# Reordering the prologue of an AdaLN block: modulation, filler matmuls, vector loads and a GpSimd subtraction

## The reference

```python
mod = (silu(c) @ wmod).reshape(4, 6, 1, 256)          # c is (4, 256), wmod is (256, 1536)
sa, ca, ga, sb, cb, gb = (mod[:, k] for k in range(6))
ga, gb = bounded(ga), bounded(gb)
h = layernorm(x) * (1 + ca) + sa
x = x + ga * mixer(h)          # first half
h = layernorm(x) * (1 + cb) + sb
x = x + gb * experts(h)        # second half: 8 experts, top 2, FFN width 1024

def mixer(x):
    xn = rmsnorm(x, norm1_w)
    left = gelu(xn @ left_W + left_b)
    u = causal_conv4(xn @ right_W + right_b)
    r, i = sigmoid(u @ ga_W + ga_b), sigmoid(u @ gx_W + gx_b)
    log_a = -8 * softplus(a_param) * r
    h = linear_recurrence(exp(log_a), sqrt(1 - exp(2 * log_a)) * i * u)
    x1 = (left * h) @ out_W + out_b + x
    x1n = rmsnorm(x1, norm2_w)
    return (gelu(x1n @ up1_W + up1_b) * (x1n @ up2_W + up2_b)) @ down_W + down_b + x1
```

## Time and profile before

| | us |
|---|---|
| median of 3 runs | 278.48 (278.12 to 279.31) |
| the profiled execution | 278.96 |
| its span, first to last instruction | 277.2 |

### The profile page before, as it was taken

How to read it: one execution, slowest core, us unless ns; L and a number is a source line. 1 busy time by engine, 2 the same in 40 slices (tenths; PEclk the granted TensorE clock), 3 DMA queues, 4 the chain that set the end, 5 groups by cost and what they waited for, 6 DMA issues and landing times.

```text
span 277.2 us, 4511 instructions
## 1 busy us (share of the span) xinstructions
PE 261.6 (94%) x1593; PEld 219.4 (79%) x1594; DVE 196.4 (71%) x459; ACT 173.7 (63%) x295; POOL 124.8 (45%) x104
## 2 busy tenths in 40 slices
PE   6989999899999999999999789999999999999991
PEld 2755655366688788877579689999999999999991
DVE  3678589919947777879947679885868677785630
ACT  4228778676189336990789557948669393958310
POOL 8140403000061302448275543877483838668454
PEclk9959999999999999999999999999999999999997
DMA  6990000000003857225277558869294875818044
GB/s 185 379 352 8 0 1 0 0 2 0 0 2 100 279 165 187 22 90 182 109 231 226 155 175 254 223 183 314 58 328 119 248 212 167 232 18 218 12 53 51
DMA packets 32838, 38.40 MB, mean 139 GB/s; under 512 B 7964, under 2 KB 28444, under 8 KB 32796
## 3 DMA queue, kind: packets, MB, share of 16 engines
q1 hardware_dynamic: 27184, 30.56, 35.6%
q0 software_dynamic: 4928, 7.44, 11.8%
q10 hardware_dynamic: 700, 0.07, 0.2%
HBM read 32.10 MB, written 8.90 MB: 148 GB/s over the span
## 4 chain that ended last, share of the span: by engine, by line
PE 63%; DVE 13%; ACT 7%; DMA 6%; issue 5%; POOL 4%; POOLq 1%; SPq 0%; DVEq 0%; ACTq 0%
PE bank L1008 18%; PE bank L1051 12%; PE bank L691 11%; PE bank L616 4%; PE bank L788 4%; POOL x_rows L2070 3%; PE bank L1045 2%; PE bank L1044 2%; DMA x_rows<-h_rows,slot_b 2%; PE bank L995 2%; DVE u L1577 2%; PE bank L627 2%; PE bank L635 1%; ACT tmp L1233 1%; DMA x_tok<-in_L_attn_x 1%
## 5 line engine op out<-in xcount | busy, mean ns | idle before, releaser
L2111 POOL DMA_INDIRECT out_x<-y_tok,meta x24 | 50.8, 2115 | 36.2 <-DVE y_tok L1938 20.9
L1051 PE MATMUL bank<-w_hi,own 128*128 128x256 f32 x256 | 48.2, 283 | 0.0
L1377 ACT ACTIVATE own_raw<-bank,b1c 128x320 f32<-128x320 f32 x64 | 33.4, 533 | 14.1 <-PE bank L1008 13.8
L1920 DVE TENSOR_TENSOR own<-own_raw,own 128x256 fp32r<-128x256 f32 x64 | 27.2, 425 | 20.0 <-ACT own L1383 19.9
L1051 PEld LDWEIGHTS bank<-w_hi,own 128*128 128x128 f32 x256 | 40.9, 191 | 0.0
L1008 PE MATMUL bank<-xe_hi,w_hi 128*128 128x320 f32 x128 | 39.9, 312 | 1.0 <-DVE xe_lo L1916 1.0
L1008 PE MATMUL bank<-xe_lo,w_hi 128*128 128x320 f32 x128 | 39.6, 309 | 0.0
L1008 PE MATMUL bank<-xe_hi,w_lo 128*128 128x320 f32 x128 | 39.6, 309 | 0.0
L1051 PE MATMUL bank<-w_lo,own 128*128 128x256 f32 x128 | 36.2, 283 | 0.0
L2101 POOL DMA_INDIRECT gb_rows<-gb_table,meta x24 | 24.9, 1037 | 12.3 <-issue 6.7
L1383 ACT ACTIVATE own<-own_raw 128x320 fp32r<-128x320 f32 x64 | 29.8, 482 | 0.0
(11 more groups left out here) (248 smaller groups left out, 606.2 us busy)
## 6 DMA issues: line engine op xcount, KB each, us to landing
e_raw<-in_L_ffn_w SPq DMA_DIRECT2D x16, 1024.0 KB, 5.8
x_rows<-in_L_attn_x SPq DMA_DIRECT2D x1, 2560.0 KB
xe_tok<-x_rows SPq DMA_DIRECT2D x7, 256.0 KB, 6.0
raw_m<-in_L_attn_up_W SPq DMA_DIRECT2D x2, 768.0 KB, 9.8
x_tok<-in_L_attn_x SPq DMA_DIRECT2D x2, 512.0 KB, 5.3
out_x<-x_tok SPq DMA_DIRECT2D x1, 1024.0 KB, 5.2
xe_tok<-x_rows SPq DMA_DIRECT2D x7, 128.0 KB, 6.2
wmod<-in_L_wmod SPq DMA_DIRECT2D x1, 768.0 KB, 11.7
```

What stands on the lines that cost most here:

```text
L1051: ins = nc.tensor.matmul(bank[b][0:n, 0:D], l, r, start=False, stop=(c == KE - 1 and t == 2))
L1377: nc.scalar.activation(own_raw[:, f % 4, :], bank[b][:, 0:CAP], ACT.Gelu, bias=b1c[:, g:g + 1]).then_inc(drained[b], 1)
L1920: nc.vector.tensor_tensor(own_lo[e % 2][:, f, :], own_raw[:, f % 4, 0:whole], own_hi[e % 2][:, f, 0:whole].bitcast(F32), ALU.subtract)
L2111: nc.gpsimd.indirect_dma_start(out_rows, bass.IndirectOffsetOnAxis(ap=ids[0:n, e, k, E:E + 1], axis=0), y_tok[e % 2][0:n, k, :], None, com ...
```

## The change

Five edits:
- Modulation: `warm(("warm", 1), ...)` moves from behind the wait for `cT` to ahead of it and has 4 fillers instead of 8; VectorE copies cT between `bn_stats` and `aggregate` instead of behind `aggregate`.
- Fillers: two between the blocks of the first mean square, two behind "vec", four instead of one behind the first `spread`.
- The even vectors are issued by ScalarE in three groups: two vectors behind a_param, two behind the sigmoid, three behind `ln_root(1)`.
- The last product of `left` of half 1 is split around `mean_square` of the second rmsnorm: its first matmul stands between the two blocks, its second behind them; `spread2(0)` comes ahead of "gb" and "b1"; one filler instead of four.
- GpSimd waits for the convolution of half 0 (`conv_done` at 2) before the first `wm_lo`.

```diff
-            def mean_square(key, hf, n):
+            def mean_square(key, hf, n, between=None):
...
+                    if between and dt == 0:
+                        between()
...
             transposes("cT", lambda j: c_row[0:B, j * P:(j + 1) * P], KD, B, step=B)
+            warm(("warm", 1), 4)
             until_drained("cT")
...
-            warm(("warm", 1), 8)
             pe.wait_ge(wmod_in, 16)
...
+            def fill(n):
+                ps = bank[order.at[("warm", 2)][0]]
+                for k in range(n):
+                    nc.tensor.matmul(ps[:], all_ones[:], all_ones[:, 0:1].to_broadcast([P, HT]), start=True, stop=True)
-            mean_square(("ms", 0), 0, 0)
+            mean_square(("ms", 0), 0, 0, lambda: fill(2))
...
             transposes("vec", lambda j: rows[0:NV, :], 1, NV)
+            fill(2)
             pe.wait_ge(rinv_done, 1)
             spread(("rb", 0), 0)
-            warm(("warm", 4), 1)
+            warm(("warm", 4), 4)
...
-            side("left", 1, 1, [1])
-            mean_square2(0)
+            left_bank, left = begin(("left", 1, 1))
+            def last_left(c):
+                return nc.tensor.matmul(left[:], raw_a[:, 1, c, P:2 * P], xn[:, c, hs[1]], start=(c == 0), stop=(c == KD - 1))
+            mean_square(("ms2", 0), 0, 2, lambda: last_left(0))
+            end(last_left(1), left_bank)
+            spread2(0)
...
-            any_w = wm_hi[:, 0]
-            spread2(0)
-            stay_busy(("busy", 5), any_w, 4)
-            wm_ready(2)
+            stay_busy(("busy", 5), wm_hi[:, 0], 1)
...
+            load_vectors(act, names[0:4:2], vec_in)
             act.wait_ge(consts_done, 2)
             act.wait_ge(c_in, 16)
             nc.scalar.activation(c_sig[0:B, :], c_row[0:B, :], ACT.Sigmoid).then_inc(sigmoid_done, 1)
+            load_vectors(act, names[4:8:2], vec_in)
...
-            load_vectors(act, names[0::2], vec_in)
+            load_vectors(act, names[8::2], vec_in)
...
-            ln_stats(x_tiles(0))
+            first_stats = bn_stats_of(x_tiles(0))
             b, ps = full("cT")
             nc.vector.tensor_copy(cT[:], ps[:, 0:KD * B].rearrange("p (k b) -> p k b", k=KD)).then_inc(drained[b], 1)
+            aggregate(x_tiles(0), first_stats)
...
+            pool.wait_ge(conv_done, KH)
             for n in range(2):
                 pool.wait_ge(wm_hi_done, n + 1)
                 lo(wm_lo[:, n], raw_m[:, n], wm_hi[:, n], wm_lo_done)
```

More of the change, by code:

```diff
@@ L1454, in bn_stats_of @@
                 return st.mark(last)
-            def ln_stats(tile):
-                aggregate(tile, bn_stats_of(tile))
             def x2_stats(hf):
```

## The result

| | before | changed |
|---|---|---|
| median of the executions beside each other | 279.23 us (278.12 to 281.45) | 277.0 us (275.72 to 280.7) |
| the profiled execution | 278.96 | 276.33 |
| its span | 277.2 | 274.6 |

The ratio is 0.9919, with a 95% interval of 0.9895 to 0.9943: faster by 0.8%, where 1.6% was forecast. The forecast of 274.1 missed by 2.9 us; 277.0 lies inside the range, close to the 276.0 of the rival in which the clock falls all the same. Of the 2.9 us, 0.75 are the level of the kernel before, whose median was 278.48 in the 3 runs shown and is 279.23 in 22; the gain was 2.2 us where 4.35 was forecast. (Ratios leave out executions over 1.5% above the fastest of their kernel, here four of the changed kernel's 22, at 280.2 to 280.7 us.)

What follows compares the result with a forecast made beforehand. It saw a sparse prologue chain, TensorE usually last, with the clock halved from 14.4 to 21.2. Gains of 0.95 + 1.0 + 1.95 = 3.9, plus 0.45, made 4.35 us: forecast 274.1, range 273.2 to 277.3.

Steps and rivals of the forecast that it cites:

- the clock falls all the same: Rival: prologue clock drops about when it did before; 277.9 us, or 276.0 if fillers bring it back; chance 0.3.
- Do they hold it?: Whether the prologue's new fillers keep the clock at full speed through spread and first side; given 0.63.
- the spread: First rmsnorm's spread, 8 matmuls: at held clock 1.05 us in place of 2.09, gaining 1.0.
- start of the spread: First rmsnorm's spread begins 0.95 us earlier, from the modulation's 1.3 less the fillers' overrun.
- the first side: First large product, 8 matmuls: at held clock about 3.5 us in place of 5.42, gaining 1.95.
- Modulation: Prologue's 16 small matmuls start about 6.8 in place of 8.22; xhat transposes end 1.3 us earlier.
- Fillers' overrun: New prologue fillers outlast their waits by about 0.25 us in the mean square and 0.1 behind "vec".
- The row that the 0.63 leaned on: Stretch at 58.2 in the kernel before: one-column matmuls mixed with wider ones, and the clock kept.
- Lock at softplus: GpSimd's moved subtraction holds softplus's first VectorE operation about 0.85 us, so half 1's gates start 0.55 late.
- GpSimd's wait: Moving the subtraction behind the convolution spares VectorE's xhat a hold that would cost at the new pace; no size.
- Second rmsnorm: Split left product and earlier spread bring xn 1.0 us earlier; 0.45 net of the late gates.
- That a gain at xn reaches the end: After the second rmsnorm VectorE carries the chain, so xn's gain, 4.35 us in all, is passed on.

Runs made afterwards that it cites:

- filled kernel: Changed kernel with seven single fillers through the first mean square in place of two, and six in place of four ahead of it: 275.13 us, ratio 0.9856.
- e4: Kernel before with only the second rmsnorm's edits (split left product, earlier spread, one filler in place of four): 278.46 us, ratio 0.9974.
- e14: Kernel before with only GpSimd's wait for the convolution ahead of the first wm_lo: 279.69 us, ratio 1.0016.
- e7: Filled kernel with the second rmsnorm back in the old order (whole left product, later spread, four fillers): 276.15 us, ratio 0.9886.
- e6: Filled kernel without GpSimd's wait for the convolution: 276.63 us, ratio 0.988.
- e11: Filled kernel with single fillers only in the first block of the first mean square, four in place of seven: 274.51 us, ratio 0.9833.
- e2: The run of the filled kernel: 275.13 us, ratio 0.9856.
- e9: The changed kernel itself, unaltered, run again for a second profile: 275.87 us, ratio 0.9873.
- e5: Changed kernel with the first mean square, root and reciprocal done 512 columns wide, no first spread, ten fillers in the wait for xn: 278.34 us, ratio 0.9961.
- e10: Kernel before with dense fillers alone, in the first mean square, ahead of it, behind vec and behind the spread: 279.23 us, ratio 0.9992.
- e3: Changed kernel without GpSimd's wait for the convolution: 277.24 us, ratio 0.9899.
- e12: Filled kernel with all seven even vectors issued behind the first root again: 276.6 us, ratio 0.9877.
- e1: Changed kernel without the prologue's new fillers (none in the mean square or behind vec, one behind the spread): 277.75 us, ratio 0.9929.

## Why the prediction was wrong

The step that failed is **"Do they hold it?"**, the 0.63 for the fillers holding the clock. They did not hold it: the clock was at 0.50 from 13.0 to 16.4, the spread took 1.71 where 1.05 was forecast, and a second fall, which was not in the forecast, took 1.71 from the gates. The terms, each as the time gained:

| step | forecast | changed kernel | filled kernel |
|---|---|---|---|
| xhat transposes done | 1.3 | 1.43 | 1.12 |
| start of the spread | 0.95 | 0.66 | 0.31 |
| the spread | 1.0 | 0.38 | 1.09 |
| from its end to the first side | 0 | -0.34 | 0 |
| the first side | 1.95 | 1.99 | 1.75 |
| **end of the first side** | **3.9** | **2.69** | **3.14** |
| from there to the gates | -0.55 | -0.21 | -0.22 |
| the gates of half 1 | 0 | -1.71 | 0 |
| gates' end to xn | 1.0 | 1.32 | 0.92 |
| **xn** | **4.35** | **2.09** | **3.84** |

- **Modulation**: right. It started at 6.89 for 6.8 and ended its transposes at 9.41 for 9.5.
- **Fillers' overrun**: the spread started at 14.07 for 13.8, and that is the clock too. The two fillers behind "vec" took 0.96, forecast at 0.44, since the clock had fallen at 13.0. With the forecast's 0.44 the spread would have started at 13.55, an estimate, so the overrun itself was not charged too low.

```profile
13.11 0.96 PE bank L684 x2
```

- **Clock**: wrong for the spread, right for the first side. This is the rival "the clock falls all the same", with the clock back by the start of the side; that the fillers brought it back is not shown (e4 and e14). Its working gave 276.0 and the profiled execution took 276.33, which is in part luck, as the parts differ: the first side's start came 0.7 earlier, not 0.1, since the spread took 1.71 and not 2.09 and the four fillers behind it 1.26 and not 1.75. The gain of 0.6 there went, with more, into the gates.
- **The second fall** was missed. The second modulation (matmuls of 4 columns) runs from 40.2 to 42.1 us, and I priced only the first stage for the clock. It took 1.71 from the gates in the profiled execution. 0.4 of it came back by xn (from the gates' end to xn 1.32 are gained in the changed kernel, 0.92 in the filled one): in the filled kernel TensorE is idle for 0.92 right behind them, in the changed one it goes straight on.
- **The row that the 0.63 leaned on** was itself a matter of the execution. The stretch at 58.2 kept the clock in the profile of the kernel before. e7 runs the same matmuls, and the same stretch lies 3.1 us earlier there. TensorE was busy throughout, and the clock fell:

```profile
55.00:58.40 3.40, 3.40 (x25) 2.52 (x24) 0.18 (x1) 2.83 (x5) 0.00 (x0) 1.00 0.00 0
58.40:61.80 3.40, 3.40 (x13) 2.63 (x12) 1.87 (x3) 1.17 (x2) 0.00 (x0) 0.50 0.02 5
```

  e14, with the same matmuls again, lost it there too, at 60.0.
- **Lock at softplus**: the mechanism is right, the size was not. The first operation took 0.87, against 0.17 before, so 0.70 in place of 0.85, and 0.2 of it reached the gates instead of 0.55. e6, where that operation took 0.17, bears this out: from the end of half 1's transposes to the gates it is 20.86 us there, 20.87 before, 21.07 changed and 21.09 filled. The changed kernel's timelines, GpSimd and VectorE:

```profile
24.98 6.82 POOL L2056 TENSOR_TENSOR wm_lo<-raw_m,wm_hi 128x1536 fp32r<-128x1536 f32 x2 [16.91 <-DVE u L1588]
...
30.96 0.87 DVE L1511 TENSOR_SCALAR lru<-lru 128x2 f32<-128x2 f32 x1 [0.34 <-ACT lru L1218]
```

- **GpSimd's wait**: right, and worth more than I said (1.5 us once the clock is held, e6; nothing in e14's median). The forecast took it as a cost avoided and never stated its size, which hid how the two parts hang together.
- **Second rmsnorm**: right, 0.93 by the chain in e4 and 0.92 in the filled kernel, 1.0 by e7's median.
- **That a gain at xn reaches the end**: right to the tenth as far as the second half's layernorm, by the 66.9 us that all profiles share. Behind it the dispatch stage scatters by 2.7 us, more than the 2.09 gained at xn, so a single execution needn't show the gain at its end.

With the clock held by denser fillers, the forecast's sum nearly comes out. Its 4.35, less the 0.64 by which the extra fillers and a modulation 0.3 later delay the spread, and with 0.33 given back from the lock, is 4.04, where 3.84 was measured; the first side gained 1.75 and not 1.95. Its time, 274.1 plus about 0.5 for the difference to 3.84, is near the 274.5 and 275.1 of e11 and e2.

On why the clock falls, I weighed the idle share too lightly and the rows of one execution too heavily. The changed kernel lost the clock, at 43.8, behind a stretch with TensorE busy for 3.04 of 3.40 us (the row from 40.6 to 44.0, above). The same kernel kept it in e9, with 3.02 busy in the same place:

```profile
40.60:44.00 3.40, 3.02 (x20) 2.33 (x19) 3.09 (x5) 3.35 (x5) 1.16 (x2) 1.00 0.00 0
```

The filled kernel kept it as well, with the same code there and 3.02 busy (39.9 to 43.3). So busy time in such a stretch does not decide it. The Trainium skill, TensorE: Matmul & The Clock Gate, section HAM oscillation, puts the drop down to gaps in which TensorE waits for data. That fits two falls, e5's at 20.7 (busy for 1.28 of 3.40 us) and e11's at 157.7 (1.41 of 3.40), though the kernel before kept its clock behind 0.88 of 3.40. It doesn't fit the one in the gates, where at most 0.36 of 3.40 us was idle, nor e7's, behind 3.40 of 3.40. What does decide between two executions of one kernel is not shown here and stays open. So does why executions of the kernel before at the same mean clock, 0.991, took 278.13 and 279.95 us. The dispatch stage (54.2 to 56.9 us) could hold that difference, and so could a start like e10's, 1.65 us at a granted clock of 1.00; those executions had no profile.

## What to carry to other kernels

When a gain hangs on the clock being held, price it over several executions and for every thin stretch of the kernel, not for the one that the profile happened to show; test it with fillers that are too many, and only then take some out. Two edits can each be worth nothing in the median and both together over half a per cent: a held clock moved TensorE up against VectorE's xhat, which GpSimd's subtraction held, and the wait alone moved something that TensorE reached late anyway. To judge an edit in a scattering kernel, look for a point behind which all profiles agree for a while, compare the starts of that point, and check that the terms ahead of the edit agree: e10's did not.

## What the runs showed of the hardware

- The granted clock is not a property of the program alone. 28 executions of the changed kernel had means from 0.969 to 0.999. In its profiles the clock fell at 13.0 and 43.8, or at 13.6 alone; in kernels that differ from it elsewhere, first at 8.0 (e3), 8.2 (e12), 8.6 (e1) or 41.6 us (e11).
- The profile's granted clock doesn't show the first microseconds. It reads 1.00 from the start, but in all profiles the fillers start 0.43 us apart up to 3.7 us (in the kernel before at 1.55, 1.97, 2.40, 2.83), the pace that they have at a granted 0.50 (two in 0.85 in e3), and in e10 they kept it up to 9.87. Later, at a granted 1.00, four took 0.87 (filled kernel, 15.42).
- A VectorE operation that met GpSimd's 128x1536 subtraction was held to its end: four xhat tiles took 4.50 us in place of 1.38, and a 128x2 operation on two elements 0.87 in place of 0.17. The RECIPROCAL of 128x4 at 26.34 in the filled kernel took 0.18 with GpSimd busy from 24.53 to 31.36, so it was not held.
- RECIPROCAL on VectorE took 3.35 us for 128x512 and 0.18 for 128x4.
